# Two-layer graph kernel: third Q and K groups ahead of O, next x split a slot sooner, layer norm dealt out over four steps, x1 rounded a slot later, and another share-out of the projection work

## The reference

```python
# layer 0, 16 heads of 32
q, k, v = x @ Wq.T, x @ Wk.T, x @ Wv.T
a = q @ k.T * 512**-0.5 + 2 * adj          # per head
o = softmax(a) @ v                          # rows of zeros give 0
x1 = layernorm(x + o @ Wo.T)
# layer 1, one of 4 experts per graph, batch norm over all graphs of an expert
top = argmax(x1.mean(rows) @ router_w + router_b)
out = adj @ (x1 @ expert_w[top])
y = layernorm(x1 + relu(batchnorm(out)))
```

## Time and profile before

| | |
|---|---|
| median of 3 runs | 2643.57 us |
| the profiled execution: its time, its span | 2645.42 us, 2643.6 us |
| PE, DVE, ACT, POOL busy | 85%, 68%, 59%, 64% of the span |
| granted TensorE clock, mean | 0.933 of 2.4 GHz |
| first step 0.0 of graph 0, last step 15.3 of graph 15 | 84.3 us, 2404.2 us |
| one graph of the loop (1 to 14), step 0.0 to step 0.0 | 145.4 us (three of them 145.7 to 147.1) |

### The profile page before, as it was taken

How to read it: one execution, slowest core, us unless ns; L and a number is a source line. 1 busy time by engine, 2 the same in 40 slices (tenths; PEclk the granted TensorE clock), 3 DMA queues, 4 the chain that set the end, 5 groups by cost and what they waited for, 6 DMA issues and landing times.

```text
span 2643.6 us, 49110 instructions
## 1 busy us (share of the span) xinstructions
PE 2248.8 (85%) x14496; PEld 1743.0 (66%) x14496; DVE 1791.4 (68%) x4607; ACT 1564.7 (59%) x3664; POOL 1695.0 (64%) x3148
## 2 busy tenths in 40 slices
PE   3678898999989898989999898989899998987443
PEld 2556676777767676767777676767677776755332
DVE  2575767677676867676766768576777667674588
ACT  0466666666666666666666666656666666653232
POOL 0678777777767777777777677777777776771000
PEclk8789999999999999999999999999999999988755
DMA  6487473755646474737566464747465564622697
GB/s 214 143 252 234 125 243 114 216 152 175 188 151 196 133 225 125 243 113 213 154 177 187 152 195 132 228 120 246 116 203 157 182 183 149 190 81 96 223 340 247
DMA packets 215346, 476.82 MB, mean 180 GB/s; under 512 B 40944, under 2 KB 49136, under 8 KB 208304
## 3 DMA queue, kind: packets, MB, share of 16 engines
q1 hardware_dynamic: 215088, 473.74, 58.3%
HBM read 272.25 MB, written 67.11 MB: 128 GB/s over the span
## 4 chain that ended last, share of the span: by engine, by line
PE 63%; DVE 16%; issue 8%; POOL 5%; ACT 4%; SPq 3%; DMA 2%; DVEq 0%; ACTq 0%; POOLq 0%
PE t_bank L346 13%; PE p_bank L259 12%; PE p_bank L260 11%; PE p_bank L261 11%; PE o_bank L365 8%; PE s_bank L329 6%; POOL fold L670 2%; DVE att L491 2%; SPq L697 2%; DVE ln_raw L1049 2%; POOL fold L672 1%; ACT att L421 1%; DVE x_lo L554 1%; POOL fold L677 1%; DVE xt L554 1%
## 5 line engine op out<-in xcount | busy, mean ns | idle before, releaser
L670 POOL TENSOR_TENSOR fold<-att 128x256 f32<-128x256 f32 x1024 | 769.3, 751 | 536.2 <-DVE nmax L491 448.4
L491 DVE CUSTOM_DVE_ANT_0 att<-s_bank,adj_t 128x512 f32<-128x512 f32 x1024 | 695.4, 683 | 421.2 <-PE s_bank L329 420.6
L421 ACT ACTIVATE att<-att,nmax 128x512 f32<-128x512 f32 x1024 | 736.7, 720 | 116.0 <-POOL fold L670 101.8
L464 ACT ACTIVATE pt<-t_bank 128x512 f32<-128x512 f32 x768 | 457.2, 595 | 498.4 <-PE t_bank L346 494.3
L346 PE MATMUL t_bank<-ident,att 128*128 128x128 f32 x4096 | 634.4, 279 | 15.8 <-DVE pt L500 8.5
L346 PEld LDWEIGHTS t_bank<-ident,att 128*128 128x128 f32 x4096 | 506.3, 143 | 198.3 <-issue 80.2
L329 PE MATMUL s_bank<-k_stack,q_stack 128*128 128x512 f32 x1024 | 490.4, 480 | 70.8 <-DVE nmax L491 70.0
L672 POOL TENSOR_TENSOR fold<-fold 128x128 f32<-128x128 f32 x1024 | 492.0, 480 | 80.3
L677 POOL TENSOR_TENSOR fold<-fold 128x64 f32<-128x64 f32 x1024 | 355.4, 347 | 80.3
L365 PE MATMUL o_bank<-pt,v 128*32 128x256 f32 x4096 | 255.0, 390 | 50.0 <-issue 38.6
L329 PEld LDWEIGHTS s_bank<-k_stack,q_stack 128*128 128x128 f32 x1024 | 199.3, 195 | 98.6 <-DVE nmax L491 93.4
(11 more groups left out here) (157 smaller groups left out, 3647.8 us busy)
## 6 DMA issues: line engine op xcount, KB each, us to landing
q_stack<-qk_t SPq DMA_DIRECT2D x1024, 64.0 KB, 3.1
k_stack<-qk_t SPq DMA_DIRECT2D x1024, 64.0 KB, 2.0
qk_w<-qk_split SPq DMA_DIRECT2D x123, 512.0 KB, 5.0
slot_a<-vo_split SPq DMA_DIRECT2D x16, 2048.0 KB, 9.5
slot_a<-expert_split SPq DMA_DIRECT2D x16, 2048.0 KB, 8.1
slot_b<-vo_split SPq DMA_DIRECT2D x15, 2048.0 KB, 8.1
stage<-in_xT SPq DMA_DIRECT2D x16, 1024.0 KB, 5.7
adj_t<-in_adj SPq DMA_DIRECT2D x64, 256.0 KB, 7.7
```

What stands on the lines that cost most here:

```text
L421: eng.activation(att[:, u % 4, j, :], att[:, u % 4, j, :], ACT.Exp, bias=nmax[:, u % 4, j:j + 1], scale=-1.0, accum_out=rsum[:, u % 4, j:j ...
L464: eng.activation(pt[:, j, :, (u % 2) * P:(u % 2 + 1) * P], t_bank[r % 2][:, :].rearrange("p (m n) -> p m n", m=NT), ACT.Copy).then_inc(act ...
L491: eng.tensor_tensor_reduce(out=att[:, u % 4, j, :], in0=s_bank[r % 2][:, :], in1=adj_t[:, t, :], scale=-2.0, scalar=3.0e38, op0=ALU.add, o ...
L670: eng.tensor_tensor(fold1[:, :], a[:, 0:256], a[:, 256:512], ALU.add).then_inc(pool_fold1, 1)
```

## The change

- `TASKS`: Q 3 moves ahead of O- 0 and K 3 ahead of O- 1. Chunks are then K 2, Q 3 (slot 2), Q 3, O- 0 (3), K 3, O- 1 (4), O- 1, O- 2 (5), O- 3 and the first of Q+ 0 (6), Q+ 0 and the first of K+ 0 (7), the rest of K+ 0 alone (8), sum- and S- 0 (9), route-, S- 1, Q+ 1 (10); S- 3 ends at 12.3 and M- 0 begins at 13.0.
- `HALF_SLOTS`: five chunks instead of four in slot 6, four instead of six in slot 7, three instead of three and a half in slot 8, 6.8 instead of 6.6 in slots 9 to 15.
- SP loads the next x at slot 3 instead of 4; ACT and DVE split it in slot 5 instead of 6.
- POOL splits adjT at 2.1, 2.2, 2.3 and 3.0.
- `dve_rstd` runs in two parts, 7 instructions at 7.0 and 6 at 7.1, and the quarters are normalised at 7.2 and 7.3, all of them after the step's tasks; ACT rounds x1 in slot 8, DVE makes its low parts at 8.3 and 9.0. On DVE an O- task's share falls at 3.3, 5.0, 5.3 and 6.2 (before: 3.0, 3.3, 5.0 and 6.1).

```diff
@@ -37,15 +37,14 @@
 
 TASKS = [
     ("V", 0), ("V", 1), ("V", 2), ("V", 3),
-    ("K", 2), ("O-", 0), ("O-", 1), ("Q", 3), ("O-", 2), ("K", 3),
-    ("O-", 3),
+    ("K", 2), ("Q", 3), ("O-", 0), ("K", 3), ("O-", 1), ("O-", 2), ("O-", 3),
     ("Q+", 0), ("K+", 0), ("sum-", 0), ("S-", 0), ("route-", 0), ("S-", 1),
     ("Q+", 1), ("S-", 2), ("K+", 1), ("S-", 3),
     ("M-", 0), ("M-", 1), ("M-", 2), ("M-", 3), ("Q+", 2),
 ]
 
 COST = {"sum-": 0.7, "route-": 0.1}
-HALF_SLOTS = [4, 4] * 2 + [3, 3] * 4 + [4, 0] + [3, 3] + [2, 1.5] + [3.3, 3.3] * 7
+HALF_SLOTS = [4, 4] * 2 + [3, 3] * 4 + [3, 2] + [2, 2] + [1.7, 1.3] + [3.4, 3.4] * 7
 
 AHEAD = [("Q+", 0), ("K+", 0), ("Q+", 1), ("K+", 1), ("Q+", 2)]
 
@@ -441,7 +440,7 @@
             has_prev, has_next, attends = kind
             work = plan(u, kind) if u >= 0 else [[]] * HG
             for j in range(HG):
-                if u == 7 and has_prev:
+                if u == 8 and has_prev:
                     wait(eng, dve_x1, b, NT, j + 1 - NT)
                     wait(eng, pe["S"], b, DT, -DT)
                     eng.activation(x1t[:, j, :], x1[:, j, :], ACT.Copy).then_inc(act_hi["X"], 1)
@@ -450,7 +449,7 @@
                         wait(eng, pe["V"], b, NT, NT if attends else 0)
                         wait(eng, ld_at, b, 16, 0)
                     eng.activation(slot_b[:, 0, j, :], stage[:, j, :], ACT.Copy).then_inc(act_at, 1)
-                if u == 6 and has_next:
+                if u == 5 and has_next:
                     if j == 0:
                         wait(eng, pe["K"], b, GROUPS, GROUPS)
                         wait(eng, pe["Q"], b, GROUPS, GROUPS)
@@ -526,27 +525,28 @@
             wait(eng, act_spread, b, PAIRS, pair + 1)
             eng.tensor_tensor(spread[:, :], o_bank[pair % 2][:, 0:256], spread[:, :], ALU.mult).then_inc(dve_scaled, 1)
 
-        def dve_rstd(eng, b):
+        def dve_rstd(eng, b, part):
 
             n = 13
-            count = [0]
+            count = [0 if part == 0 else 7]
 
             def link(ins):
                 count[0] += 1
                 ins.then_inc(dve_newton, 1)
                 wait(eng, dve_newton, b, n, count[0] - n)
-            wait(eng, dve_ln, b, 8, 0)
-            link(eng.tensor_scalar(ln_var, ln_mv[:, :, 1], EPS, None, ALU.add))
-            link(eng.tensor_scalar(ln_half.bitcast(I32), ln_var.bitcast(I32), 1, None, ALU.logical_shift_right))
-            link(eng.tensor_copy(ln_std, ln_half.bitcast(I32)))
-            link(eng.tensor_scalar(ln_rstd.bitcast(I32), ln_std, -1.0, float(0x5f3759df), ALU.mult, ALU.add))
-            for _ in range(3):
+            if part == 0:
+                wait(eng, dve_ln, b, 8, 0)
+                link(eng.tensor_scalar(ln_var, ln_mv[:, :, 1], EPS, None, ALU.add))
+                link(eng.tensor_scalar(ln_half.bitcast(I32), ln_var.bitcast(I32), 1, None, ALU.logical_shift_right))
+                link(eng.tensor_copy(ln_std, ln_half.bitcast(I32)))
+                link(eng.tensor_scalar(ln_rstd.bitcast(I32), ln_std, -1.0, float(0x5f3759df), ALU.mult, ALU.add))
+            for _ in range(1 if part == 0 else 2):
                 link(eng.scalar_tensor_tensor(out=ln_half, in0=ln_var, scalar=-0.5, in1=ln_rstd, op0=ALU.mult,
                                               op1=ALU.mult))
                 link(eng.tensor_tensor(ln_half, ln_half, ln_rstd, ALU.mult))
                 link(eng.scalar_tensor_tensor(out=ln_rstd, in0=ln_half, scalar=1.5, in1=ln_rstd, op0=ALU.add,
                                               op1=ALU.mult))
-            assert count[0] == n
+            assert count[0] == (7 if part == 0 else n)
 
         def dve_low(eng, dst, src, hi, scale=1.0):
 
@@ -637,23 +637,23 @@
                         wait(eng, act_ot, b, PAIRS, pair + 1)
                         dve_low(eng, ot[:, 1, g, half * 256:half * 256 + 256], spread[:, :],
                                 ot[:, 0, g, half * 256:half * 256 + 256]).then_inc(dve_ot, 1)
-                if (u, j) == (6, 2) and has_prev:
-                    dve_rstd(eng, b)
-                if (u, j) in ((6, 3), (7, 0)) and has_prev:
-                    for t in (0, 1) if j == 3 else (2, 3):
-                        eng.tensor_scalar(x1[:, t, :], x1[:, t, :], ln_mv[:, t, 0:1], ln_rstd[:, t:t + 1],
-                                          ALU.subtract, ALU.mult).then_inc(dve_x1, 1)
-                if u == 8 and j in (1, 2) and has_prev:
-                    if j == 1:
+                if (u, j) in ((8, 3), (9, 0)) and has_prev:
+                    if j == 3:
                         wait(eng, act_hi["X"], b, NT, 0)
                         wait(eng, st_x1, b, 16, 0)
-                    for t in (2 * j - 2, 2 * j - 1):
+                    for t in (0, 1) if j == 3 else (2, 3):
                         dve_low(eng, x1_lo[:, t, :], x1[:, t, :], x1t[:, t, :]).then_inc(dve_lo["X"], 1)
                 for task, c in work[j]:
                     if c == 3:
                         dve_task(eng, b, task, kind)
                         if task[0] == "route-":
                             dve_choose(eng, b)
+                if u == 7 and has_prev:
+                    if j < 2:
+                        dve_rstd(eng, b, j)
+                    for t in {2: (0, 1), 3: (2, 3)}.get(j, ()):
+                        eng.tensor_scalar(x1[:, t, :], x1[:, t, :], ln_mv[:, t, 0:1], ln_rstd[:, t:t + 1],
+                                          ALU.subtract, ALU.mult).then_inc(dve_x1, 1)
 
 
         def pool_slot(eng, b, u, kind, kind_before):
@@ -676,8 +676,8 @@
                         wait(eng, dve_total_done, b, UNITS, uu - 1)
                     eng.tensor_tensor(fold2[:, uu % 2, jj, :], fold1[:, 0:P // 2], fold1[:, P // 2:P],
                                       ALU.add).then_inc(pool_fold2, 1)
-                if u in (2, 3) and j % 2 == 1 and has_prev:
-                    t = 2 * (u - 2) + j // 2
+                t = 4 * (u - 2) + j - 1
+                if 0 <= t < NT and has_prev:
                     wait(eng, act_at, b, NT, t + 1 - NT)
                     eng.tensor_tensor(slot_b[:, 1, t, :], stage[:, t, :], slot_b[:, 0, t, :].bitcast(F32),
                                       ALU.subtract).then_inc(pool_at, 1)
@@ -717,7 +717,7 @@
                 wait(eng, st_mixed, b, 16 * DT, -16 * DT)
                 wait(eng, dve_bn, b, BN_OPS, -BN_OPS)
                 eng.dma_start(x1[:, :, :], dram(x, b, -1).rearrange("(t p) n -> p t n", p=P)).then_inc(ld_x, 16)
-            if u == 4 and has_next:
+            if u == 3 and has_next:
                 wait(eng, pool_at, b, NT, 0)
                 wait(eng, act_xt, b, DT, DT)
                 wait(eng, dve_xt, b, DT, DT)
```

## The result

The changed kernel takes 2759.4 us (2756.66 to 2762.39) where the kernel before takes 2644.28 us: ratio 1.0436, 95% interval 1.042 to 1.0451. It is slower, as forecast, but by 115 us and not by 49; the range that I gave ended at 2738 us.

The account below looks back on a forecast made before the run. PE was taken as the bound in slots 0 to 4 and 10 to 15, DVE's full queue in 5 to 9. +1.6 +1.0 +0.95 -0.1 = +3.45 us a graph, x 14 = 48, graph 15 +1: 2693 us; range 2622 to 2738.

Parts of the forecast that it names:

- DVE's queue: Slots 5 to 9: 37.35 us occupied plus 6.25 us of waits; last low part 4.1 us later, step 10.0 +1.6 us.
- the waits at 6.1 and 8.2: DVE idles 2.0 us after slot 5's PV block and 2.25 us at 8.2 for K+ 0's rounding.
- the one wait of 4.33 us for 2.0: After the PV block of slot 7, DVE was forecast to wait 2.0 us for its next logits.
- I take 0: Half clock behind PE's idle time at 9.0: between 0 and 1.3 us, taken as 0, with 1.3 kept for the range.
- Rival 3: Clock falls at 9.0, or at 7.3's waits too: +1.3 to +2.5 us a graph more, 2711 to 2728 us; chance 0.22.
- The late slots: From step 10.0 on: +1.0 us for one chunk and the router, +0.95 us for M- 0's wait, per graph.
- The moved chunk and router: At 10.0, S- 1's first chunk (0.7) and the router (0.3) are still to do where PE is the bound: +1.0 us.
- M- 0: S- 3 ends at 12.3, its low part behind DVE's weights; PE waits 1.7 us for 0.79 before: +0.95 us.
- Slot 3, -0.1: Slot 3 gains as DVE loses an O- task there: -0.1 us a graph, bounds 0 and -0.3.
- GpSimd and SP, 0: POOL's adjT splits in adjacent steps, SP's earlier x load (1.4 us of cover) and its stacks and stores cost 0.
- Dealing out the chain, 0: On DVE in slots 5 to 9, the layer norm's chain is the same work in another order: 0 us.
- The rule on shared interfaces: GpSimd contends with DVE instructions having two SBUF inputs: all four x splits 0.9 in slot 5, +0.7 us a graph; not adopted.

Follow-up runs that it names:

- the fills: The changed kernel with overwritten matmuls in TensorE's three idle stretches: before the last scores and PV block of slots 5 and 7, and before sum-; 2707.5 us.

## Why the prediction was wrong

By its own steps, for graph 7:

- **DVE's queue, right.** Its start of slot 5's work, at 2.85 us after PE's, and the waits at 6.1 and 8.2 came within 0.5 us, its occupied time within 0.6. The last low part was forecast 46.3 us after step 5.0 and came 48.2 after it (1241.49 less 1193.32); 42.2 before. The excess is the one wait of 4.33 us for 2.0, less what the other terms came short; with the clock held that wait is 1.87 us. With the clock held by the fills, slots 5 to 9 take 53.7 us, and I had forecast 54.0.
- **Clock, wrong.** The step that failed is "I take 0". The clock was priced at 0 to 1.3 us and only at 9.0. It costs 3.9 us a graph (52 us in all, by the run with three fills): 1.8 us in slots 7 and 8, where the PV block takes 3.64 us and DVE waits for it, 0.9 in slot 9, and 1.2 in slots 5 and 6, from the graphs whose slot 5 runs below full clock. The reason that I gave for 0, that the resumed work is paced by DVE, does not hold: behind a PV block DVE waits for PE, as the forecast's own wait of 2.0 us there says. Rival 3 named the mechanism, at 2711 to 2728 us, with the size too small by 1.4 us a graph and more. Graph 11 of the kernel before, 1.7 us longer with one PV block at half clock, stood in the trace, and the prediction does not use it.
- **The late slots, right in kind, short in size.** The moved chunk and router cost 1.4 us (slots 10, 11 and 14) for 1.0 forecast. M- 0 cost 1.26 us (slot 13 up by 2.29, slot 12 down by 1.03) for 0.95. Together 2.7 for 1.95. That S- 3's low part stands behind the weights is 0.9 of the 1.26, by the run that moves it.
- **Slot 3, -0.1:** 0. **GpSimd and SP, 0:** right, by the run with the splits put back. **Dealing out the chain, 0:** right for DVE, wrong by 2.9 us through the clock (part of the 3.9).
- **The rule on shared interfaces** (the Trainium skill, GPSIMD Engine Reference, Key points)**:** the four splits of graph 7 lasted 0.81, 0.78, 0.95 and 0.72 us. From the start of each to the next instruction they took 0.73, 0.71, 0.87 and 0.65, mean 0.74, which is the mean that I took (0.73) and not the 0.9 of the dearer case; the rule was not what was missed.

Sum for the mean loop graph: 8.0 us for 3.45. Of the 4.55 more, 3.9 is the clock and 0.7 the late slots. One further part was not tried: the layer norm left where it was with the rest of the change, because x1's rounding in slot 7 would then have to wait for a later step of its own ring.

## What to carry to other kernels

When one engine's queue is full over a stretch, taking away the longest wait that another engine shows there moves the wait to the next point of the ring; count the full engine's work first, and look where it still idles. Where the clock may fall in a PE wait, price the work behind that wait at half clock too, above all if another engine waits for it: here matmuls whose results are overwritten, put into the waits, made the changed kernel 52 us faster. And judge an edit by the slot that it touches as well as by the total, and look at the granted clock of every graph and not of one: a clock that is on the edge can hide a gain, or add to it.

## What was not expected of the hardware

- Nearly the same waits of PE in the same order of work ended at either clock: 2.11 and 1.96 us at half clock (slot 7 of graph 2 of the run with the chain in one go, slot at 0.78, PV block 3.63 us), 2.09 and 2.46 us at full clock (graph 7 of it, slot at 1.00, PV block 1.93 us).
- The same slot of the same program was at clock 1.00 in one graph and 0.82 in the next (slot 5, graphs 7 and 8 of the changed kernel), and took 1.7 us more. An edit in slot 9 or 13 changed in how many graphs slot 5 was slow. What sets this phase stays open.
